# A two-layer network in one kernel: the last feed-forward and attention follow the linear attention two steps closer

## The reference

```
x = x + attn_a_L0(layernorm(x));  x = x + ffn_L0(layernorm(x))
x = x + attn_b_L0(layernorm(x));  x = x + ffn_L0(layernorm(x))
x = x + linear_attention(layernorm(x))   # q, k through a feature map elu(.)+1, 16 heads
x = x + swiglu(layernorm(x))             # silu(x Wg) * (x Wu), then Wd; 384 hidden
x = x + causal_attention(layernorm(x))   # 16 heads of 8 channels
x = x + swiglu(layernorm(x))
```

## Time and profile before

| | us |
|---|---|
| median of 3 runs (4345.05 to 4351.43) | 4350.73 |
| the profiled execution | 4349.36 |
| its span, first to last instruction | 4347.4 |
| TensorE busy | 4061.2 (93%) |
| VectorE busy | 3351.6 (77%) |
| ScalarE busy | 2915.0 (67%) |
| GpSimd busy | 2390.7 (55%) |

### The profile page before, as it was taken

One profiled execution on the slowest core, in us unless ns is written; L12 is line 12 of the kernel. 1 busy time (PEld: TensorE's weight loads), 2 busy tenths in 40 slices (PEclk: granted clock), 3 DMA queues, 4 the chain that ended last, 5 costly groups with the idle time before them and its releaser, 6 DMA issues. The chain is left out here.

```text
span 4347.4 us, 128585 instructions
## 1 busy us (share of the span) xinstructions
PE 4061.2 (93%) x53847; PEld 2019.5 (46%) x53847; DVE 3351.6 (77%) x5020; ACT 2915.0 (67%) x7325; POOL 2390.7 (55%) x1684
## 2 busy tenths in 40 slices
PE   5998999999999999998979999999999999987897
PEld 3223555545555554553435555455554555543443
DVE  3776888888888888885658888888888888865664
ACT  2765777777777777774557777777777777755554
POOL 3314766666666666664227666667666666641120
PEclk7999999999999999998999999999999999999998
DMA  4121000000000000001220000000000000000110
GB/s 166 57 60 31 2 22 7 2 21 7 22 7 2 22 7 2 2 2 57 64 65 2 2 21 7 21 7 4 24 2 21 7 2 2 2 10 18 50 58 8
DMA packets 68917, 97.79 MB, mean 22 GB/s; under 512 B 34472, under 2 KB 58756, under 8 KB 62340
## 3 DMA queue, kind: packets, MB, share of 16 engines
q1 hardware_dynamic: 67476, 83.28, 6.4%
q10 hardware_dynamic: 864, 6.29, 0.4%
HBM read 72.18 MB, written 16.78 MB: 20 GB/s over the span
## 5 line engine op out<-in xcount | busy, mean ns | idle before, releaser
L402 POOL TENSOR_TENSOR ra<-ra,rb 128x1024 f32<-128x1024 f32 x384 | 927.7, 2416 | 328.7 <-DVE rb L741 328.6
L416 POOL TENSOR_TENSOR qkr<-ra,inv 128x1024 f32<-128x1024 f32 x384 | 731.3, 1904 | 612.7 <-ACT inv L680 609.0
L448 PE MATMUL ps<-wvo,xs 128*32 128x512 f32 x6144 | 820.9, 606 | 72.3 <-ACT vs L602 72.3
L493 PE MATMUL ps<-wq,xs 128*128 128x512 f32 x1536 | 749.7, 611 | 7.2 <-DVE rb L741 4.5
L653 ACT ACTIVATE pr<-ps,neg 128x64 f32<-128x64 f32 x3072 | 670.3, 338 | 7.1 <-DVE neg L718 7.1
L602 ACT ACTIVATE vs<-ps 128x512 f32<-128x512 f32 x768 | 451.2, 588 | 226.7 <-PE ps L448 225.7
L515 PEld LDWEIGHTS ps<-kt,qt 64*32 64x32 f32 x24576 | 359.6, 107 | 293.2 <-issue 290.3
L718 DVE TENSOR_REDUCE neg<-ps 128x8 f32<-128x512 f32 x384 | 263.7, 687 | 279.2 <-PE ps L515 272.7
L493 PEld LDWEIGHTS ps<-wq,xs 128*128 128x128 f32 x1536 | 275.6, 192 | 434.7 <-issue 335.9
L738 DVE TENSOR_TENSOR ra<-ps,rope 128x1024 f32<-128x1024 f32 x384 | 451.8, 1177 | 23.4 <-ACT sq L627 16.2
L1505 DVE TENSOR_REDUCE nm<-ps 128x1 f32<-128x512 f32 (+3 forms) x768 | 378.3, 549 | 117.6 <-PE ps L1270 115.2
(11 more groups left out here) (251 smaller groups left out, 6203.4 us busy)
## 6 DMA issues: line engine op xcount, KB each, us to landing
wq<-in_L_ffn_Wqkv SPq DMA_DIRECT2D x12, 1024.0 KB, 5.2
wvo<-wvo_scratch SPq DMA_DIRECT2D x12, 1024.0 KB, 4.8
wvo_scratch<-pt ACTq DMA_DIRECT2D x6, 1024.0 KB, 4.1
w<-in_L_ffn_W SPq DMA_DIRECT2D x12, 341.0 KB
qs<-norm_pieces SPq DMA_DIRECT2D x9, 384.0 KB
ks<-norm_pieces SPq DMA_DIRECT2D x9, 384.0 KB
qs<-latent_pieces SPq DMA_DIRECT2D x9, 384.0 KB
ks<-latent_pieces SPq DMA_DIRECT2D x9, 384.0 KB
```

Source lines behind the costliest of these rows:

```text
L402: pool.tensor_tensor(ra[:, m % 2, :, :], ra[:, m % 2, :, :], rb[:, :, :], ALU.add).then_inc(sum_done.sem, 1)
L416: pool.tensor_tensor(qkr[:, m % 2, :, :].rearrange("p s (h c) -> p (s h) c", c=HD), ra[:, m % 2, :, :].rearrange("p s (h c) -> p (s h) c", ...
L448: last = pe.matmul(VP[32 * j:32 * j + 32, :], xs[:, turn % 2, v * WIN:v * WIN + WIN], wvo[l % 2][:, j, :], start=True, stop=True)
L493: last = pe.matmul(PJ[:, qk, :], xs[:, turn % 2, t * P:t * P + P], wq[l % 2][:, at:at + 512], start=True, stop=True)
```

## The change

One constant, the start of the join of `swiglu_1` into `linear`. `LIN_FIRST` is -6, so the guest starts after 4 host steps in place of 6, beside the linear step -2. Its step k stands behind the linear step k + 14, in place of k + 16, and `plain` and `swiglu_2` keep their distance to it.

```diff
-INTO_SWIGLU = (-LIN_FIRST, (1,))
+INTO_SWIGLU = (-LIN_FIRST - 2, (1,))
 INTO_PLAIN = (10 - SW_FIRST, (1,))
 INTO_LAST = (30 - PLAIN_FIRST, (1,))
```

## The result

The changed kernel takes 4366.61 us in the median of 6 runs (4361.11 to 4368.57), the kernel before 4345.76 us in 6 runs beside it (4340.54 to 4351.43). The ratio is 1.0047, with a 95% interval from 1.0034 to 1.0059: slower by 0.47%, some 20 us. The profiled execution took 4367.04 us with a span of 4365.0, 17.6 us above the span before. Forecast were +16.5 us, a median of 4367. That the median agrees to 0.4 us is luck in part: the kernel before took 5 us less beside it than in the three runs from which the forecast counted, and the difference is 20 us, not 16.5.

A forecast was written before the change was run, and what follows sets the result against it. TensorE's work plus the waits its written order exposes was taken to bound the stage; batches 0 to 3 (1.2 + 3.2 + 4.8 + 5.3 = 14.5 us) and clock (+2) gave +16.5, so 4367 us, range 4351 to 4380.

The forecast's parts named there:

- The back of batch 1: Linear attention's batch 1, from feature tile F3's end to the next projection: 28.6 us against 25.5; with the front, +3.2 us.
- the front: Start of a period up to F3's end: two gates more, same two latencies, 0.1 us dearer for batch 1.
- Batch 2: Period with the last attention's first row: key projection L1218 waits about 3 us for the query's copy; +4.8 us.
- Batch 3: Period with the last attention's second row: query L1215 waits 6.9 us for L1535 behind L2017; +5.3 us.
- Batch 0: Beside the second block's last feed-forward: weight turning L1928 moves two steps earlier and waits about 1.75 us; +1.2 us.
- The clock: Half clock after the added TensorE pauses, with about 5 us before L1699 in each period: +2 us (0 to +8).
- one of my signs of being wrong: After the first scores of the last attention: a change in length there would show the forecast wrong.
- the rival in which it decides: Each 5 us pause puts the two projections and values behind it to half clock: +22.3 us, 4373; chance 0.15.
- The waits: TensorE's waits over the three periods: a rise from 23.5 to about 40 us (11.8 + 13.3 + 15.2).
- the waits behind the wide passes: TensorE behind ScalarE's early sigmoid passes: F6 some 2.7 us (batch 1), L1218 3 to 4 (batch 2), L1215 6 to 7 (batch 3).
- the rival "waits only change places": Each period loses under 1 us and the pause before L1699 shortens by the same: +2 us, 4353; chance 0.14.
- The faster rival: Earlier passes pull each period forward: -8.4 us, 4342; decided by O2 starting less than 17.6 us after F3; chance 0.09.

The follow-up runs named there:

- the twelve profiles: One profile per timed kernel, before and change included; batch 0 averages 52.9 us with the feed-forward's weight turning at its old place, 54.85 with it early.
- The filler: The change plus four unread 512-wide TensorE products ahead of the last L1699, inside its 3.46 us wait; 1.0035 to the kernel before.
- one-pass kernels: First feed-forward's three wide ScalarE passes cut to one Exp (sigmoid not computed): in the kernel before 0.9974, in the change 1.0015, both to the kernel before.
- the two runs on L1962: Down projection L1962 moved alone: two steps later in the change, 1.0003; one step earlier in the kernel before, 1.0041; both to the kernel before.

## Why the prediction was right

**The back of batch 1** came within 0.6 us up to L1699. Counted from the end of F3 (3950.34 after the change): F6's wait 2.28 us (said 2.7), L1962 at 17.7 (17.25), O2 at 20.4 (19.85), L1699 at 28.3 (27.7), the projection at 30.0 (28.6, at full clock). From O2 to L1699 it is 7.84 us, as the working had it (19.85 to 27.7), where the 8.7 of before were called the same; the wait of 5.10 us that was forecast is there. The period grew by 2.2 us, not 3.2: the front was cheaper, since the down projection of the second block's feed-forward covered the latency ahead of gate 0 and the variance waited 0.55 us.

**Batch 2**, said +4.8, gave +4.4. L1218 waited 2.27 us, not 3 to 4, because TensorE had already stood 1.29 us ahead of the query for L1535, which I had not written down.

**Batch 3**, said +5.3, gave +6.4: L1215 waited 5.92 us (6.9 said), L1962 3.01, and L1962 ran at half clock.

**Batch 0**, said +1.2, gave +1.4, and +1.9 over the twelve profiles; L1928 waited 2.19 us.

**The clock**, said +2 within 0 to 8, gave 3.2 us behind the last L1699 alone, where I had written that nothing would change from L1942 on. A change in length behind the first scores was one of my signs of being wrong, and it came: 280.2 us from the first score (L1269) to the end, in place of 277.9. The step that missed is the one that let the effect of the pauses end at the last L1699. The filler shows that the 3.2 us are half clock granted after the pause ahead of it. The projections behind the pauses of batches 1 and 2 took 2.76 and 3.62 us, each 1.88 before: 2.6 us more. Taken net, with what the half clock had cost before, TensorE is busy for 111.7 us in the three periods in place of 109.1, and for 3.1 us more behind the last L1699. So the clock cost some 5.7 us, nearer to the 7.8 of the rival in which it decides than to my +2, and the 20 us by the ratio lie between my 16.5 and its 22.3. The rule that I cited from the Trainium skill, "TensorE: Matmul & The Clock Gate", section on HAM oscillation, that each such pause is paid for at the restart, agrees with these rows, though not behind each pause: with L1962 two steps later TensorE waited 2.53 us in batch 1, and L1699 and L1719 behind it took 1.13 and 1.88 us, full clock.

**The waits** rose less than said: 34.1 us, not 40. The working did not agree with itself here. With the same products at full clock the periods should grow by what the waits grow, but it has +13.3 us for the periods (3.2, 4.8, 5.3) and +16.8 for the waits (23.5 to 40.3). Measured were 10.6 us of waits and 2.7 of clock, together near the 13.1 by which the periods grew. The sum came out near because waits put too high and a clock put too low made up for each other; that is luck. The direction, the waits of F6 and L1215 and the pause ahead of L1699 (5.1, 4.2 and 3.5 us; about 5 was said for each) are not.

**The sizes of the terms were off.** I spread the loss over the waits behind the wide passes and over L1962. The pair of one-pass kernels and the two runs on L1962 give almost all of the loss to L1962: a group of three pairs with its own wait, set ahead of the outputs that VectorE's last chain needs. For the waits behind the passes the rival "waits only change places" was the right one. The faster rival fell at the point named for it: O2 started 20.4 us after F3, past the 17.6.

## What to carry to other kernels

When a guest's instructions move in a woven order, look for the group that waits longest and ask which of the host's products it now stands ahead of: if a short chain of another engine hangs on those, the wait and the group's own time both go onto the path, and the group no longer covers that chain. Hand-timing one period engine by engine from trace rows gave each batch's share here to 1.1 us, clock included; the chain of waits alone pointed the wrong way. The guest stretched (early parts early, its last product late) lost nothing that the interval shows: 1.0003 (0.9994 to 1.0012).

## What the runs showed of the hardware

TensorE's grant was at half behind waits of 2.2 us (L1962 before, 4.37 us in place of 2.84) to 5.9 us (L1215), but not behind each (the 2.53 us ahead of L1699 in the run with L1962 later). From the last L1699 on it cost 3.1 us; 3.6 us of useless products in such a pause won it back (284.4 us to 281.1 from the last L1699 to the end). Single profiles differ by up to 3 us in stretches whose order is the same (batch 0: 52.1 to 55.1 us), so a term of 1 us needs several of them.
